# Column norms from squares in two 16-bit parts, made on GpSimd, and placed one projection later

## What is computed

```python
q = _causal_conv_silu(x @ Wq, qcw, qcb).reshape(b, t, HK, DK)   # 16 heads of 128
k = _causal_conv_silu(x @ Wk, kcw, kcb).reshape(b, t, HK, DK)
v = _causal_conv_silu(x @ Wv, vcw, vcb).reshape(b, t, HK, VE)   # VE = 256
q = _l2norm(q)                       # x / max(norm(x), 1e-12)
k = _l2norm(k)
alpha, beta = sigmoid(x @ Wa), sigmoid(x @ Wb)
# per token: state = a*state; err = v - state^T k; state += b * k err^T; out = state^T q
```

## Time and profile before

| | us |
|---|---|
| median of 3 runs | 1176.99 |
| lowest and highest | 1175.23, 1182.03 |
| the profiled execution | 1187.94 |
| its span, first to last instruction | 1186.1 |

### The profile page before, as it was taken

One profiled execution on the slowest core, in us unless ns is written; L12 is line 12 of the kernel. 1 busy time (PEld: TensorE's weight loads), 2 busy tenths in 40 slices (PEclk: granted clock), 3 DMA queues, 4 the chain that ended last, 5 costly groups with the idle time before them and its releaser, 6 DMA issues.

```text
span 1186.1 us, 24906 instructions
## 1 busy us (share of the span) xinstructions
PE 1057.7 (89%) x8176; PEld 714.3 (60%) x8176; DVE 844.3 (71%) x1427; ACT 721.0 (61%) x1284; POOL 442.2 (37%) x574
## 2 busy tenths in 40 slices
PE   3589999999999999999899999998887889996987
PEld 3257777777777776777677677776554334443444
DVE  4768888877888877888688788877544656663354
ACT  3367777777776776767677676776332345555221
POOL 5254544535445453553435355436201122223000
PEclk9889999999999999999999999999997679998788
DMA  6002000010000000000000100000000040000001
GB/s 182 20 1 63 2 28 28 1 28 0 27 27 1 27 0 27 27 0 27 3 28 1 28 27 0 10 1 1 1 1 1 1 75 1 2 2 22 1 1 36
DMA packets 30359, 22.44 MB, mean 19 GB/s; under 512 B 3014, under 2 KB 29318, under 8 KB 30139
## 3 DMA queue, kind: packets, MB, share of 16 engines
q1 hardware_dynamic: 27547, 16.89, 4.9%
q0 software_dynamic: 2720, 4.42, 1.8%
HBM read 22.94 MB, written 1.05 MB: 20 GB/s over the span
## 4 chain that ended last, share of the span: by engine, by line
PE 61%; DVE 13%; ACT 12%; issue 10%; POOL 1%; DVEq 1%; DMA 1%; SPq 0%; ACTq 0%; POOLq 0%
PE psum L1121 10%; PE psum L1179 5%; DVE y L877 4%; PE psum L1147 4%; PE psum L1260 4%; PE psum L1298 3%; PE psum L1273 3%; PE psum L1199 3%; ACT L648 2%; PE psum L1137 2%; PE psum L1207 2%; PE psum L1457 2%; ACT kq L648 2%; ACT sq L651 2%; DVE ux L842 2%
## 5 line engine op out<-in xcount | busy, mean ns | idle before, releaser
L434 POOL TENSOR_TENSOR ct<-lm,levels 128x512 f16<-128x512 f32 x224 | 253.1, 1160 | 261.1 <-DVE lm L887 261.1
L877 DVE SCALAR_TENSOR_TENSOR y<-psum,cwh,y 128x508 f32<-128x508 f32 (+2 forms) x384 | 284.4, 741 | 17.6 <-ACT y L604 8.6
L842 DVE TENSOR_TENSOR ux<-ux,psum 128x512 f16<-128x512 f16 x192 | 130.7, 681 | 46.5 <-PE psum L1208 46.4
L1137 PE MATMUL psum<-wo,vt 128*128 128x256 f32 x512 | 127.4, 393 | 1.9 <-DVE y L877 1.4
L604 ACT ACTIVATE y<-psum,cwh 128x512 f32<-128x512 f32 x128 | 99.0, 774 | 37.7 <-PE psum L1121 37.7
L579 ACT ACTIVATE t1c<-psum 128x256 f16<-128x256 f32 x192 | 73.1, 380 | 63.0 <-PE psum L1199 61.9
L724 ACT ACTIVATE et<-psum 128x1024 f32<-128x1024 f32 x64 | 65.6, 1025 | 62.6 <-PE psum L1442 62.5
L1137 PEld LDWEIGHTS psum<-wo,vt 128*128 128x128 f32 x512 | 94.5, 195 | 12.8 <-DVE y L877 1.6
L991 DVE TENSOR_REDUCE mx<-psum 128x4 f32<-128x1024 f32 x64 | 77.7, 1221 | 28.8 <-PE psum L1421 28.6
L1199 PE MATMUL psum<-ux,ct 128*128 128x128 f16 x768 | 97.5, 221 | 0.6 <-ACT t1c L579 0.6
L856 DVE TENSOR_TENSOR ux<-ux,psum 128x512 f16<-128x512 f16 x128 | 87.6, 685 | 14.3 <-PE psum L1208 11.8
(11 more groups left out here) (209 smaller groups left out, 2346.0 us busy)
## 6 DMA issues: line engine op xcount, KB each, us to landing
wraw<-in_L_attn_Wv SPq DMA_DIRECT2D x32, 128.0 KB, 2.7
wo<-in_L_attn_Wo SPq DMA_DIRECT2D x16, 256.0 KB, 2.8
wraw<-in_L_attn_Wk SPq DMA_DIRECT2D x16, 128.0 KB, 2.5
wraw<-in_L_attn_Wq SPq DMA_DIRECT2D x16, 128.0 KB, 2.7
x<-in_x SPq DMA_DIRECT2D x8, 128.0 KB, 5.2
maskrow<-in_mask_row POOLq DMA_DIRECT2D x1, 1024.0 KB, 4.6
xt<-in_ctx SPq DMA_DIRECT2D x1, 1024.0 KB, 6.0
out<-x SPq DMA_DIRECT2D x8, 128.0 KB, 1.8
```

What stands on the lines that cost most here:

```text
L434: g.tensor_tensor(ct[:, st.c % 4, l], lm[:, st.c % 4, :, 0, :], levels[:, l, :].unsqueeze(1).to_broadcast([P, NB, T]), ALU.mult).then_inc( ...
L842: v.tensor_tensor(u, u, pr, ALU.subtract).then_inc(uxb_sb, 1)
L877: v.scalar_tensor_tensor(out=y[:, n, :, sh:], in0=u[:, :, 0:T - sh], scalar=cwh[:, (a.c // 2) % 2, n, TAPS - 1 - sh:TAPS - sh], in1=y[:, n ...
L1137: mm = t.matmul(ubank[n][:, j * H:(j + 1) * H], vt[:, r, vc, (2 * n + j) * T:(2 * n + j + 1) * T], wo[:, hr, vc, :], start=(vc == 0), stop ...
```

## The change

Five edits. (1) ACT still squares, now with a scale of 4 before the square (so 16 times as much), into the same 32-bit tile. (2) POOL gets split_sq as its last call of the slot: it waits for the squares and makes sqh, their 16-bit rounding, and sql, the 16-bit rest, each over 128x1024. (3) PE's norms take 16 matmuls in 16 bits (sqh and sql summed in PSUM) in place of 8 in 32 bits, wait for split_sq, and stand behind proj_(0). turn moves behind proj_(1). floor undoes the factor 16. (4) On DVE floor moves from behind level_b(0, 0) to behind level_c(4, 0), and terms behind taps(0). On ACT logs moves behind bias(0), rowcopy behind bias(1). (5) ct has 2 buffers instead of 4, so that cut for a step waits for the last level product of the step two before it, not four.

PE at the start of an ordinary slot, before: zz products, norms, level products, first projection (xth, xtl with whi, wlo), then b_ux(1, 0).

The diff, without two new semaphores, one wait at the end of POOL's loop and the index of ct in b_first:

```diff
@@ -166,7 +166,7 @@
         identb = lb("identb", [P, P], BF16)
         select = lb("select", [P, 12, P], BF16)
         ident64 = lb("ident64", [P, P], F32)
-        ones = lb("ones", [P, 1], F32)
+        ones = lb("ones", [P, 1], F16)
         gz = lb("gz", [P, B * 2 * HK], F32)
         ga = lb("ga", [P, B * 2 * HK], F32)
         gl = lb("gl", [P, B, 2 * HK], F32)
@@ -185,6 +185,8 @@
         kq = lb("kq", [P, 2, NB, 2, T], F32)
         vt = lb("vt", [P, 2, 2, TOK], F32)
         sq = lb("sq", [P, NB, 2, T], F32)
+        sqh = lb("sqh", [P, NB, 2, T], F16)
+        sql = lb("sql", [P, NB, 2, T], F16)
         n2m = lb("n2m", [P, 2, NB], F32)
         lnn = lb("lnn", [P, 2, NB], F32)
         rc = lb("rc", [P, 12], F32)
@@ -193,7 +195,7 @@
         rows = lb("rows", [P, P], BF16)
         decay = lb("decay", [P, NB, 2, T], F32)
         lm = lb("lm", [P, 4, NB, 2, T], F32)
-        ct = lb("ct", [P, 4, LEVELS, NB, T], F16)
+        ct = lb("ct", [P, 2, LEVELS, NB, T], F16)
         ux = lb("ux", [P, 2, NB, 2, T], F16)
         t1b = lb("t1b", [P, NB, T], F16)
         t1c = lb("t1c", [P, NB, T], F16)
@@ -422,16 +425,27 @@
             pool.wait_ge(xn_done, B)
             split(0, 0, None)
             def slot(k):
-                b, b0 = k, k.at(1)
+                a, b, b0 = k.at(2), k, k.at(1)
+
+                def split_sq():
+
+                    if not a.valid():
+                        return
+                    pool.wait_ge(squared, a.count(1, 1))
+                    need(pool, norm_psum, a.count(1, 0))
+                    f, hi, lo = [q[:].rearrange("p j a t -> p (j a t)") for q in (sq, sqh, sql)]
+                    g.tensor_tensor(hi, f, zero[:].to_broadcast([P, NB * 2 * T]), ALU.add).then_inc(sq_high, 1)
+                    pool.wait_ge(sq_high, a.count(1, 1))
+                    g.tensor_tensor(lo, f, hi, ALU.subtract).then_inc(sq_split, 1)
 
                 def cut(st, levels_):
 
                     if not st.valid():
                         return
                     pool.wait_ge(lm_done, st.count(2, 2))
-                    need(pool, t1c_psum, st.at(-4).count(6, 6))
+                    need(pool, t1c_psum, st.at(-2).count(6, 6))
                     for l in levels_:
-                        g.tensor_tensor(ct[:, st.c % 4, l], lm[:, st.c % 4, :, 0, :],
+                        g.tensor_tensor(ct[:, st.c % 2, l], lm[:, st.c % 4, :, 0, :],
                                         levels[:, l, :].unsqueeze(1).to_broadcast([P, NB, T]), ALU.mult).then_inc(masked, 1)
 
                 cut(b, range(2, 4))
@@ -452,6 +466,7 @@
                     split(nxt.head, (nxt.c // 2) % 2, None if first else nxt.at(-4))
                 cut(b, range(4, LEVELS))
                 cut(b0, range(0, 2))
+                split_sq()
                 if k.i is None and k.c == STEPS - 3:
                     pool.wait_ge(ctx_loaded, 16)
                     pool.wait_ge(xattn_loaded, 16 * 8)
@@ -647,8 +663,8 @@
                     need(act, kq_psum, a.at(-2).count(2, 2))
                     s.activation(kq[:, r].rearrange("p j a t -> p a j t"), y[:, 0:2], ACT.Silu).then_inc(silu, 1)
                     act.wait_ge(silu, a.count(2, 1))
-                    need(act, norm_psum, a.count(1, 0))
-                    s.activation(sq[:], kq[:, r], ACT.Square).then_inc(squared, 1)
+                    need(act, sq_split, a.count(1, 0))
+                    s.activation(sq[:], kq[:, r], ACT.Square, scale=4.0).then_inc(squared, 1)
 
                 def v_silu():
                     if not a.valid():
@@ -675,17 +691,17 @@
                 zcopy(0)
                 ccopy(4, 0)
                 bcopy(1, 0)
-                logs()
                 ccopy(4, 1)
                 bias(0)
+                logs()
                 first_norm()
                 bcopy(1, 1)
                 zcopy(1)
                 k_split(0)
                 ccopy(5, 0)
                 bcopy(2, 0)
+                bias(1)
                 rowcopy()
-                bias(1)
                 k_split(1)
                 bcopy(2, 1)
                 exp(0)
@@ -898,7 +914,7 @@
                     if b0.valid():
                         dve.wait_ge(norm_psum, b0.count(1, 1))
                         need(dve, norm_ln, b0.count(1, 0))
-                        v.tensor_scalar(n2m[:].rearrange("p a j -> p (a j)"), normp, 1e-24, None, ALU.max).then_inc(norm_sb, 1)
+                        v.tensor_scalar(n2m[:].rearrange("p a j -> p (a j)"), normp, 1.0 / 16, 1e-24, ALU.mult, ALU.max).then_inc(norm_sb, 1)
 
                 def terms():
 
@@ -931,12 +947,12 @@
                                                in1=ubank[hh], op0=ALU.mult, op1=ALU.add).then_inc(k_stack, 1)
 
                 level_b(0, 0)
-                floor()
                 level_b(0, 1)
                 level_b(1, 0)
+                level_c(4, 0)
+                floor()
+                taps(0)
                 terms()
-                level_c(4, 0)
-                taps(0)
                 if k.i is None and k.c == STEPS:
                     moments(dve, 1, slice(0, NB))
                 level_b(1, 1)
@@ -1140,11 +1156,13 @@
                 def norms():
                     if not b0.valid():
                         return
-                    pe.wait_ge(squared, b0.count(1, 1))
+                    pe.wait_ge(sq_split, b0.count(1, 1))
                     need(pe, lm_done, b0.count(2, 0))
                     for kind in range(2):
                         for j in range(NB):
-                            mm = t.matmul(normp[:, kind * NB + j:kind * NB + j + 1], sq[:, j, kind, :], ones[:], start=True, stop=True)
+                            o = normp[:, kind * NB + j:kind * NB + j + 1]
+                            t.matmul(o, sqh[:, j, kind, :], ones[:], start=True, stop=False)
+                            mm = t.matmul(o, sql[:, j, kind, :], ones[:], start=False, stop=True)
                     mm.then_inc(norm_psum, 1)
 
                 def turn():
@@ -1196,7 +1214,7 @@
                     pe.wait_ge(masked, st.count(7, level + 1))
                     need(pe, sb_sem, st.count(6, n - 1))
                     for jj in range(2):
-                        mm = t.matmul(dst[:, jj * P:(jj + 1) * P], ct[:, st.c % 4, level, 2 * hf + jj], ux[:, st.c % 2, 2 * hf + jj, 1], start=True, stop=True)
+                        mm = t.matmul(dst[:, jj * P:(jj + 1) * P], ct[:, st.c % 2, level, 2 * hf + jj], ux[:, st.c % 2, 2 * hf + jj, 1], start=True, stop=True)
                     mm.then_inc(psum_sem, 1)
 
                 def both(st, hf, dst, t1s, sb_sem, n, x_sem, x_n, psum_sem):
@@ -1329,11 +1347,11 @@
 
                 b_first(0)
                 z(0)
-                norms()
                 c_t1(4, 0)
                 b_first(1)
                 b_t1(1, 0)
                 proj_(0)
+                norms()
                 b_ux(1, 0)
                 b_t1(1, 1)
                 c_t1(4, 1)
@@ -1342,10 +1360,10 @@
                 kv(0)
                 c_ux(4, 1)
                 b_ux(1, 1)
-                turn()
                 c_t1(5, 0)
                 b_t1(2, 0)
                 proj_(1)
+                turn()
                 b_ux(2, 0)
                 b_t1(2, 1)
                 c_ux(5, 0)
```

More of the change, by code:

```diff
@@ L274, in build @@
         proj, biased, tapped, silu = [sem(n) for n in ("proj", "biased", "tapped", "silu")]
+        sq_high, sq_split = sem("sq_high"), sem("sq_split")
         squared, norm_psum, norm_sb, norm_ln, rc_done, part_step, rows_psum, rows_sb = [sem(n) for n in (
@@ L471, in _ @@
             pool.wait_ge(squared, STEPS)
+            pool.wait_ge(norm_psum, STEPS)
             pool.wait_ge(masked, STEPS * LEVELS)
@@ L1188, in b_first @@
                     for jj in range(2):
-                        cj = ct[:, b.c % 4, 0, 2 * hf + jj]
+                        cj = ct[:, b.c % 2, 0, 2 * hf + jj]
                         t.matmul(bx[:, jj * 256:jj * 256 + P], ident16[:], cj, start=True, stop=True)
```

## The result

The changed kernel took 1236.99 us in the median of 4 runs (1229.85 to 1245.52), the kernel before 1179.51 (1175.23 to 1191.79). The ratio is 1.047, with a 95% interval from 1.036 to 1.058; the medians lie 57 us apart. The forecast was 1241, in a range from 1214 to 1270.

What follows compares the result with a forecast made beforehand. The prediction took PE, with hardly any slack and just about waiting for ACT's square at the norms, as the bound. Terms of 1.6 and 0.75 us a slot summed to 64 us: 1177 + 64 = 1241 us, range 1214 to 1270.

Steps and rivals of the forecast that it cites:

- What bounds: At the norms, PE just about waits for ACT's square; PE has hardly any slack, no waits behind the exponents.
- The casts: POOL's two casts take 1.894 and 2.136 us, so the norms' input is ready 4.3 us after S, the square's end.
- The first term: From the square's end to b_ux(1, 0): PE waits 1.5 us for POOL's casts at the norms; +1.6 us a slot.
- The second term: From b_ux(1, 0) to the exponents: ACT's order, then rowcopy coming last, delay PE; +0.75 us a slot.
- The sum: 24 ordinary slots at +2.3, five behind a loop boundary at +1.6, one at +1: 64 us in all.
- Rival 1: Smaller loss: one-column products nearly free or second stretch absorbed behind the exponents; 1.45 to 1.6 a slot, 1216 to 1221; chance 0.15.
- The clock: Rival 2: PE's idle stretches lower its clock, each ordinary slot losing another 1.4 us; 1275 us; chance 0.08.
- PE's busy time as the bound: Rival 3: faster, the slot loses what PE's list loses, 0.9 us in 31 slots; 1149 us; chance 0.04.
- The ring: Two ct buffers: cut waits for c_t1(6, 1), over 5 us before the masks; put at nothing.

Runs made afterwards that it cites:

- e2: The kernel before with only the changed kernel's order on PE, DVE and ACT; 32-bit norms, no casts, ring of 4: 1.048 of before.
- e5: The kernel before in the changed kernel's order, squares in one 16-bit part written by ACT, no casts: 1.023 of before.
- e10: The changed kernel with POOL's first cast only; the second part sql and its 8 products left out: 1.024 of before.
- e3: The changed kernel with casts and 16-bit norms, but all five moved calls back at their old places: 1.088 of before.
- e4: The kernel before, its order kept, ACT writing the squares in one 16-bit part, rest left out, no casts: 0.983 of before.
- e1: The kernel before with the ring of ct cut from 4 to 2 and nothing else: 0.998 of before.
- e9: The changed kernel with norms behind z(1), the chain behind moved on, one table set for logarithm and exponential, loaded in ACT's idle time: 0.996 of before.
- e7: The changed kernel with both casts, but norms moved behind z(1) and the chain behind them moved on too: 1.033 of before.
- e6: The changed kernel with the logarithm's table, which also holds the exponential, loaded in ACT's idle time ahead of ccopy(4, 1): 1.035 of before.

## Why the prediction was right

- **What bounds.** Right. PE's norms start 0.05 us behind the square, and all that delays them or what stands behind them lengthens the slot. In the changed kernel the stretch behind the exponents kept its 15.2 us. One premise for this was wrong: the forecast said that PE has no waits behind the exponents, and it has one of some 0.5 us in 30 slots, ahead of the last products of the slot, for DVE's addition to x. It is as long after as before, so nothing was caught up there:

```profile
PE psum L1298 <- DVE x L894: 14.3, 30, 0.8
```
```profile
PE psum L1316 <- DVE x L910: 14.3, 30, 0.8
```

- **The casts.** 1.89 and 2.12 us in the median of 32, as in the weight split (one of the second kind took 2.98). The norms start at S + 4.2, forecast S + 4.3.
- **The first term** was forecast at 1.6 and is 1.04. The term that was mis-sized is the price of a 16-bit product with one column: 16 take 0.42 us (554.05 to 554.47), 0.026 each, where I took 0.055 from products with 128 columns. That is 0.5 us a slot. The page of the Trainium skill that the prediction names, TensorE: Matmul & The Clock Gate, section on the weight-path perf modes, pointed the right way with its faster load of 16-bit weights, and its 40 ns, which it gives for 8-bit ones, was still more than the 26 measured here. PE waits 1.2 rather than 1.5: proj_(0) starts at S + 1.57, forecast 1.45, its last product ends at S + 3.0, forecast 2.75, and the norms start 0.1 earlier. There is also a wait that the old norms had hidden and that I had not seen, 0.41 us of c_t1(4, 0) for DVE's addition to x. It costs nothing, because proj_(0) behind it waits for zcopy(0) in any case.
- **The second term** was forecast at 0.75 and is 0.85, with the waits where they were placed: 0.78 in front of b_ux(1, 1), 0.37 for rowcopy. It comes from the order and is there without casts (e2, e5, e10).
- **The sum.** The 24 ordinary slots became 1.89 us longer on average, 45 us, for 55 forecast (24 times 2.3). The five at the loop boundary took 3 us more together in the profiled executions, where 8 was forecast, but they vary by more than that. The first two slots, put at nothing, took 3 more. That is 51 us from the first square's end to the last, for 64 forecast. The last norms came 54.3 us later (821.25 and 875.54). The span rose by only 44.5, because what follows, nearly all of it the other two sub-layers, was 9.8 us shorter in that execution, at a higher granted clock:

```profile
882.00:1186.00 304.00, 253.79 (x2150) 0.84 0.07 14
```
```profile
936.00:1230.00 294.00, 243.99 (x2142) 0.87 0.07 14
```

  (before above, after below: a stretch of PE up to the span's end, with its granted clock.) The medians are 57 us apart. So the total came nearer to the forecast than the terms did, and that part is luck: no trace shows where the 6 us between 51 and 57 lie.
- **The rivals.** Rival 1, a smaller loss, was half right: the one-column products were nearly free, and the measured 1.89 us a slot lies between its 1.45 to 1.6 and the forecast's 2.3. Its other half, a stretch absorbed behind the exponents, did not happen. The clock did not fall in ordinary slots (granted clock 1.00 in all that lie in the loop); e3 shows that it does where PE stands 4.3 us. PE's busy time as the bound fell with e4, where 1.6 us of PE work was worth 0.85. The ring cost nothing (e1).

What the forecast did not say, though its own numbers held it, is that the order alone would cost all of the loss. It speaks of the wait for the casts as the first term; but in the new order the norms come behind proj_(0), and there even the old 32-bit products without any cast put b_ux(1, 0) at S + 4.56.

## What to carry to other kernels

Find the instruction that another engine releases just in time, and count what stands behind it in the queue: work moved off the busy engine gains nothing if its substitute, here two passes in a row on another engine, ends after that point. A step that is moved must be followed to the last of its consumers, table loads included. With the same casts this kernel was 9% slower in the old order (e3), 5% slower in the new one, and as fast as before in a third with one table load fewer (e9). With the norms behind z(1), one table set for two functions, loaded in an idle stretch, gave 1.5 us a slot (e7 to e9), more than the 0.85 of the matmuls that e4 saved; in the changed kernel it gave 0.5 (e6).

## What the runs showed of the hardware that I had not expected

**One-column products with 16-bit weights** start 0.026 us apart with their 128x128 weight loads, against 0.055 for those with 128 columns and 0.113 for a 32-bit record with one column.

**Slots at the loop boundary** take from 25.6 to some 31 us, more than the ordinary ones except in e3, and by how much changes from kernel to kernel and within one execution. In the waits view of the one-cast kernel (e10) PE idles there for nothing that the profile shows (its first products of a slot, L1205):

```profile
PE psum L1205 <- issue: 14.1, 5, 3.1
```

In the kernel before the same product of b_first, L1190, has one such wait, of 4.19 us:

```profile
568.03 0.29 PE L1190 MATMUL psum<-ct,ident 128*128 128x128 f16 x1 [4.19 <-issue]
```

A part of the length is the clock. In e10, behind waits of 2.55 and 1.67 us in one such slot, PE's clock falls to its lower level for most of six us (window, us, busy, granted clock, DMA, GB/s):

```profile
586.00:592.00 6.00, 5.91 (x39) 0.62 0.01 3
```

Over a whole boundary slot of some 31 us the granted clock is 0.85 to 0.89 (e1, e5, e7, e10), over the ordinary slots of the loop 0.99 to 1.00.

The kernels e5 and e10 have boundary slots of about 31 us four times of five, and lose by it more than by their ordinary slots. What decides this was not settled: it stands at the branch of the hardware loop, and no run here varied the loop.
